# Reordering the second half's routing in a fused mixer and mixture-of-experts kernel, with full-height spread matmuls in the first four groups

## The reference

```
z     = layernorm(layernorm(x))
proj  = (z @ lrp_w.T + lrp_b) * mask * sigmoid(z @ gate_w.T + gate_b)
left, right = split(proj)
tri   = einsum('bikc,bjkc->bijc', left, right)
x1    = x + tri + sigmoid(tri @ og_w.T + og_b) * (layernorm(tri) @ op_w.T + out_bias)
t     = layernorm(x1)
p     = softmax(t @ router_w + router_b);  top 2 of 8, renormalised
out   = x1 + sum over the two of p_e * (t @ expert_w[e] + expert_b[e])
```

## Time and profile before

| | us |
|---|---|
| median of 3 runs (lowest, highest) | 144.69 (143.39, 145.44) |
| the profiled execution's own time | 144.41 |
| its span, first to last instruction | 142.6 |
| busy in the span: TensorE, VectorE, ScalarE, GpSimd | 123.1, 103.6, 76.9, 75.7 |
| mean granted TensorE clock | 0.964 of 2.4 GHz |

### The profile page before, as it was taken

How to read it: one execution, slowest core, us unless ns; L and a number is a source line. 1 busy time by engine, 2 the same in 40 slices (tenths; PEclk the granted TensorE clock), 3 DMA queues, 4 the chain that set the end, 5 groups by cost and what they waited for, 6 DMA issues and landing times. The chain is left out here.

```text
span 142.6 us, 2140 instructions
## 1 busy us (share of the span) xinstructions
PE 123.1 (86%) x708; PEld 53.8 (38%) x711; DVE 103.6 (73%) x173; ACT 76.9 (54%) x136; POOL 75.7 (53%) x73
## 2 busy tenths in 40 slices
PE   5999788999999699889799899695899669989970
PEld 2425145767679565344134443123121111212210
DVE  0096948787774699999918994462978995989951
ACT  4168473565413359898853349858256454474400
POOL 6001033799900089989930173063552974869970
PEclk9999999999999999999999999999559996999999
DMA  4997000000000000000000899987188978871112
GB/s 90 321 350 320 0 0 5 0 0 2 0 5 0 0 2 0 0 5 0 0 0 9 186 208 205 210 187 170 26 202 202 215 182 197 199 283 74 74 74 78
DMA packets 6171, 14.55 MB, mean 102 GB/s; under 512 B 1392, under 2 KB 1648, under 8 KB 6160
## 3 DMA queue, kind: packets, MB, share of 16 engines
q1 hardware_dynamic: 6160, 14.41, 38.1%
HBM read 3.85 MB, written 2.10 MB: 42 GB/s over the span
## 5 line engine op out<-in xcount | busy, mean ns | idle before, releaser
L429 POOL TENSOR_TENSOR work<-work,late_sb 128x512 f32<-128x512 f32 x12 | 15.0, 1274 | 9.7 <-ACT work L526 9.7
L627 ACT ACTIVATE wcopy<-ps 128x512 f32<-128x512 f32 x24 | 13.6, 597 | 9.1 <-PE ps L1024 9.0
L791 PE MATMUL ps<-w1m,xk 64*128 64x256 f32 x128 | 16.2, 391 | 0.8 <-DVE xk L1103 0.3
L1024 PE MATMUL ps<-w3F,selb 32*128 32x512 bf16 x64 | 12.0, 412 | 4.0 <-DVE prod L1306 2.7
L441 POOL TENSOR_TENSOR work<-tri,stats 128x512 f32<-128x512 f32 x8 | 8.8, 1114 | 11.6 <-DVE stats L1172 11.4
L526 ACT ACTIVATE work<-ps 128x512 f32<-128x512 f32 x16 | 9.6, 597 | 9.0 <-PE ps L791 9.0
L491 POOL TENSOR_TENSOR prod<-wcopy,lr 128x512 f32<-128x512 f32 x6 | 8.3, 1405 | 11.3 <-ACT wcopy L627 8.6
L791 PEld LDWEIGHTS ps<-w1m,xk 64*128 64x128 f32 x128 | 11.6, 186 | 5.5 <-DVE lr L1118 2.4
L1118 DVE TENSOR_TENSOR lr<-ps,work 128x512 f32<-128x512 f32 x16 | 10.6, 687 | 2.5 <-POOL work L429 2.5
L1089 DVE TENSOR_SCALAR xk<-ps,head_sb 128x512 f32<-128x512 f32 x8 | 6.4, 798 | 7.4 <-ACT triF L510 7.2
L1024 PEld LDWEIGHTS ps<-w3F,selb 32*128 32x128 bf16 x64 | 3.0, 93 | 20.4 <-issue 6.6
(11 more groups left out here) (136 smaller groups left out, 257.2 us busy)
## 6 DMA issues: line engine op xcount, KB each, us to landing
lr<-triF SPq DMA_DIRECT2D x32, 128.0 KB, 2.3
xi<-in_x_F SPq DMA_DIRECT2D x8, 256.0 KB, 4.6
tri<-triF SPq DMA_DIRECT2D x16, 128.0 KB, 2.4
xk<-triF SPq DMA_DIRECT2D x16, 128.0 KB, 2.3
out<-xi SPq DMA_DIRECT2D x8, 256.0 KB, 2.1
late_sb<-in_late SPq DMA_DIRECT2D x1, 914.0 KB, 7.6
choice_sb<-in_choice SPq DMA_DIRECT2D x1, 336.5 KB, 7.8
early_sb<-in_early SPq DMA_DIRECT2D x1, 257.0 KB, 5.5
```

Source lines behind the costliest of these rows:

```text
L429: pool.tensor_tensor(unit_gates(u), unit_gates(u), mask[:, first_tokens(u)].unsqueeze(1).broadcast_to([P, 2 * C, 8]), ALU.mult).then_inc(s ...
L627: act.activation(wcopy[:, a * W:(a + 1) * W], ps[:, HELD + POOL_N[a] % 4, :], ACT.Copy)\
L791: m = pe.matmul(ps[:, unit_bank(u) + b, 2 * F1 * q:2 * F1 * (q + 1)], xk[rows, at:at + P], w1[rows, 2 * F1 * b:2 * F1 * (b + 1)], start=Tr ...
L1024: pe.matmul(ps[:, HELD + n % 4, :], selb[slot_rows(n % R), n * P:(n + 1) * P], col(w3F, g)[slot_rows(n % R), :], start=True, stop=True).th ...
```

## The change

- tri_squares of groups 4 to 7 run as one block, then x1_copy(1), tri_root(1), x1_copy(3). turn_root(1) and spread_root(1) move ahead of logits(0) and logit_bias(0). spread_root signals for each group instead of once for four.
- VectorE runs tri_scaled(4 to 7) as one block ahead of the comparisons; the gated updates lie each one place earlier between the routing steps.
- The first rounding of half 0 goes ahead of load_roots on ScalarE. TensorE issues out_gate(7) ahead of update(6) and update(7). x1_copy(7) goes from ScalarE to VectorE.
- TensorE's order from turn_weights(1, ...) on is new: all spreads of group 0 and 1 and both sums of group 0 stand ahead of pair_differences(1), and turn_weights(3) is a call of its own. RING follows. VectorE, ScalarE and GpSimd take the products and copies of groups 1 to 3 earlier between the steps of the second half.
- The spreads of groups 0 to 3 take all 128 rows of selb and w3F, those of groups 4 to 7 still 32 rows.

```diff
-                ("g", 7), ("z", 4), ("z", 5), ("z", 6), ("z", 7), ("w", 0), ("var", 1), ("logit", 1), ("w", 1),
-                ("w", 2), ("w", 3), ("std", 1), ("p", 4), ("p", 5), ("p", 6), ("p", 7), ("wins", 1), ("back", 1),
-                ("lead", 1), ("y", 0), ("y", 1), ("w", 4), ("w", 5), ("y", 2), ("y", 3), ("w", 6), ("w", 7), ("y", 4),
+                ("z", 4), ("g", 7), ("z", 5), ("z", 6), ("z", 7), ("w", 0), ("w", 1), ("w", 2), ("w", 3), ("var", 1),
+                ("logit", 1), ("std", 1), ("y", 0), ("p", 4), ("p", 5), ("p", 6), ("p", 7), ("wins", 1), ("back", 1),
+                ("lead", 1), ("y", 1), ("w", 4), ("w", 5), ("y", 2), ("y", 3), ("w", 6), ("w", 7), ("y", 4),
...
-        X1_COPIED_BY_VECTOR = [1, 3, 5]
+        X1_COPIED_BY_VECTOR = [1, 3, 5, 7]
...
             product(0, *POOL_N)
+            product(1, *POOL_N[0:2])
             root_of_each(1)
-            for g in range(1, G):
+            product(1, *POOL_N[2:3])
+            for g in range(2, G):
...
             out_gate(7)
+            round_part(0, 0)
             load_roots()
-            round_part(0, 0)
             x1_square(4)
...
             x1_square(6)
+            w3_copy(0)
             x1_copy(6)
-            w3_copy(0)
             x1_square(7)
-            x1_copy(7)
             weights_copy(0, 0)
+            w3_copy(1)
             weights_copy(0, 1)
             x1_std(1)
-            w3_copy(1)
             weights_copy(0, 2)
             logit_copy(1)
             w3_copy(2)
+            weights_copy(1, 0)
             w3_copy(3)
-            weights_copy(1, 0)
             weights_copy(1, 1)
+            weights_copy(1, 2)
+            weights_copy(2, 0)
             root_back_copy(1)
-            weights_copy(1, 2)
             load_gates()
             probabilities(1)
-            weights_copy(2, 0)
             weights_copy(2, 1)
...
                 for g in range(HG):
-                    m = pe.matmul(ps[:, HELD + g, :], lcp("slot")[slot_rows(g), :], rootF[h][slot_rows(g), :],
-                                  start=True, stop=True)
-                m.then_inc(s_rb, 1)
+                    pe.matmul(ps[:, HELD + g, :], lcp("slot")[slot_rows(g), :], rootF[h][slot_rows(g), :],
+                              start=True, stop=True).then_inc(s_rb, 1)
...
             variance(0)
+            turn_root(1)
             logits(0)
-            turn_root(1)
+            spread_root(1)
             logit_bias(0)
-            spread_root(1)
             pair_differences(0)
...
             lead(0)
+            out_gate(7)
             update(6)
             update(7)
-            out_gate(7)
...
-                    pe.matmul(ps[:, HELD + n % 4, :], selb[slot_rows(n % R), n * P:(n + 1) * P],
-                              col(w3F, g)[slot_rows(n % R), :], start=True, stop=True).then_inc(s_wb, 1)
+
+                    rows = slice(0, P) if g < HG else slot_rows(n % R)
+                    pe.matmul(ps[:, HELD + n % 4, :], selb[rows, n * P:(n + 1) * P], col(w3F, g)[rows, :],
+                              start=True, stop=True).then_inc(s_wb, 1)
...
             spread(0, 2, 3)
+            turn_weights(1, 2)
             variance(1)
+            spread(0, 4, 5, 6, 7)
             logits(1)
-            spread(0, 4, 5, 6, 7)
             logit_bias(1)
-            turn_weights(1, 2, 3)
-            turn_std(1)
             spread_first(1)
             spread(1, 2, 3)
+            turn_std(1)
+            turn_weights(3)
+            spread(1, 4, 5, 6, 7)
+            sum_experts(0, 0)
+            sum_experts(0, 1)
             pair_differences(1)
-            spread(1, 4, 5, 6, 7)
+            spread_first(2)
+            spread(2, 2, 3)
             turn_root_back(1)
             wins(1)
-            sum_experts(0, 0)
+            sum_experts(1, 0)
             lead(1)
-            sum_experts(0, 1)
-            for g in range(2, G):
+            spread(2, 4, 5, 6, 7)
+            sum_experts(1, 1)
+            for g in range(3, G):
...
-                dve.wait_ge(s_rb, g // HG + 1)
+                dve.wait_ge(s_rb, g + 1)
...
-            tri_squares(4)
-            tri_squares(5)
+            for g in range(4, G):
+                tri_squares(g)
             x1_copy(1)
-            tri_squares(6)
-            tri_squares(7)
+            tri_root(1)
             x1_copy(3)
-            tri_root(1)
...
-            tri_scaled(4)
-            tri_scaled(5)
+            for g in range(4, G):
+                tri_scaled(g)
             for n in range(HG):
                 compared(n)
             x1_root(0)
-            tri_scaled(6)
+            gated_update(4)
             top_two(0)
-            tri_scaled(7)
-            gated_update(4)
+            gated_update(5)
             lead_scaled(0)
             top_two_roots(0)
-            gated_update(5)
+            gated_update(6)
             weigh(0)
-            gated_update(6)
+            gated_update(7)
             remainder(0, 0)
-            gated_update(7)
+            closed(7)
             remainder(0, 1)
-            closed(7)
             x1_copy(5)
-            product(0, *VECTOR_N)
-            product(1, *VECTOR_N[0:2])
+            product(0, VECTOR_N[0])
+            x1_copy(7)
+            product(0, *VECTOR_N[1:5])
+            product(1, *VECTOR_N)
             x1_root(1)
+            add_x1(0)
             for n in range(HG, G):
                 compared(n)
-            product(1, VECTOR_N[2])
             top_two(1)
-            product(1, *VECTOR_N[3:5])
+            product(2, *VECTOR_N[0:2])
             lead_scaled(1)
             top_two_roots(1)
-            add_x1(0)
+            product(2, VECTOR_N[2])
             weigh(1)
-            product(2, *VECTOR_N[0:2])
+            add_x1(1)
+            product(2, VECTOR_N[3])
             remainder(1, 0)
-            product(2, *VECTOR_N[2:4])
+            product(2, VECTOR_N[4])
+            product(3, VECTOR_N[0])
             remainder(1, 1)
-            product(2, VECTOR_N[4])
-            add_x1(1)
-            product(3, *VECTOR_N)
+            product(3, *VECTOR_N[1:5])
```

## The result

The changed kernel takes 148.34 us (median of 4 runs, 147.65 to 148.94), the kernel before 144.24 in the same comparison: ratio 1.029, interval 1.024 to 1.035, slower. The profiled execution took 148.84 us with a span of 147.0, against 144.41 and 142.6.

A forecast was written before the change was run, and what follows sets the result against it. Product engines are nearly full from group 4 on, so group 4's start, set by second-half routing, decides: 3.9 less 3.0 plus 0.25 plus 0.3 is 1.45, about 145.9 us; range 142.6 to 148.4.

The forecast's parts named there:

- a rival that didn't come about: Slower side: clock falls in the first stretch too, at 100.85 to 104.9; plus 2.5, 148.4 us, chance 0.20.
- to group 4: From the last rounding's end to group 4's first product: 6.05 us instead of 5.75, plus 0.3.
- The frame: Last stage from group 4's first product stays 18.33 us; the change can only move when group 4 starts.
- The walk's steps: Four engines' queues carried forward instruction by instruction with earlier durations; group 4 starts at 123.3 instead of 121.83.
- The clock at 100: Full-row matmuls hold the clock, so pair_differences(1) to lead_scaled(1) takes 5.9 us instead of 8.87: minus 3.0.
- minus 0.5: First half: first rounding ahead of the table load, so first weights reach w3F at 90.65 instead of 91.11.
- come out even: First half: pair_differences(0) and the comparisons end at 79.0 both before and after the change.
- difference at pair_differences(1): Second half's routing: pair_differences(1) starts at 103.2 instead of 99.30, plus 3.9, with the earlier 0.5 gain used up.
- To the last rounding ... plus 0.25: From lead_scaled(1) to the last rounding's end: 8.15 us instead of 7.9, with add_x1(1) ahead of remainder(1,0).
- Never falls: Clock stays full after 90, group 4 starts near 121.9: plus 0.1, 144.5 us, chance 0.15.
- the order gave less, not more: Rival that order gives more: waits ahead of pair_differences(1) not paid, start about 100.5; 141.0 us, chance 0.12.
- The drains: TensorE ahead of pair_differences(1): five layout switches at about 0.14 us, 0.7 us of the 3.9.

The follow-up runs named there:

- kernel 12: The kernel before with full-row spreads in groups 0 to 3 and half 0's first rounding ahead of out_gate(7) and the table load: 142.66 us, ratio 0.986.
- kernel 6: The changed kernel with 15 matmuls on ones added between group 3's first spreads and ahead of turn_weights(4,5): 146.04 us, ratio 1.009.
- Kernel 1: The changed kernel with all spreads back on 32 rows: 148.28 us, ratio 1.026 to before.
- kernel 7: The changed kernel with VectorE's add_x1(1) moved behind remainder(1,0) and product(2,7), product(3,1) behind remainder(1,1): 146.00 us, ratio 1.008.
- kernel 2: The kernel before with only the spreads of groups 0 to 3 on all 128 rows: 142.99 us, ratio 0.989.
- kernel 10: The changed kernel with add_x1(1) late and 9 added matmuls, none directly ahead of turn_weights(4,5): 144.89 us, ratio 1.002.
- kernel 14: The kernel before with full rows, early first rounding, early group 1 spreads, plus the changed order ahead of the pairs (logits(1) late): 142.25 us, ratio 0.985.
- kernel 4: The changed kernel with pair_differences(1) ahead of both sums of group 0, and comparisons ahead of add_x1(0): 151.15 us, ratio 1.033.
- kernel 13: The kernel before with full rows, early first rounding, and group 1's spreads ahead of turn_std(1): 141.00 us, ratio 0.976.
- kernels 8: The changed kernel with 15 matmuls added around group 3's first spreads and add_x1(1) late: 146.89 us, ratio 1.016.
- kernels 11: The kernel before, 32-row spreads, with 22 matmuls added: 7 ahead of turn_std(1), 15 around group 3's first spreads: 145.50 us, ratio 1.002.
- kernel 9: The changed kernel with 15 added matmuls, add_x1(1) late, and 32-row spreads in all groups: 149.00 us, ratio 1.031.

## Why the prediction was wrong

The forecast was 145.9 us, within 2% of before (0.68 of the chances); the kernel is slower by 2.9%, and its time, 148.34, lies just inside the range's upper end of 148.4. That end was the price of a rival that didn't come about, so the agreement is luck. The step that failed is the term "to group 4", above all the spreads of group 3 priced at full clock. Point by point:

- **The frame held.** The end is group 4's start plus 18.33 us, to the hundredth. The walk's steps through the queues are in the trace, VectorE's wait at add_x1(1) (112.7 forecast, 114.07 found) and turn_std(1) waiting for w3_copy(2) (98.2; 99.45) among them.
- **The clock at 100.** Right: it stays up with full rows, and pair_differences(1) to lead_scaled(1) shrinks by 2.78 us, forecast 3.0.
- **"minus 0.5", gates and rounding.** Wrong in sign: w3F of group 0 came 0.68 us later (91.79). 0.33 of this was there before the first changed instruction (60.78 against 60.45). The first half's logits stand behind spread_root(1): the comparisons started 0.52 us later from the first tri_scaled, where I had written "come out even". From there to w3F only 0.17 was gained; kernel 12, with the rounding ahead of out_gate(7) too, gains 0.37. With the 0.5 us that I had counted on, this makes 1.1 us of the 3.0 us missed, almost all of the difference at pair_differences(1) (5.12 for 3.9).
- **"To group 4 ... plus 0.3".** This term failed most: 1.94, so 1.64 missed. That the clock would fall again was right, and kernel 6 shows it is the cause. The size was not: I let the clock return ahead of the spreads of group 3. It stayed at 0.50 for 6.4 us, and the full-row spreads, which I had priced at 0.22 each, cost 1.89 us together, with sums of 1.94 and 1.88 on either side. The price of the full rows was taken at full clock, while the same text placed them behind the fall of the clock. Kernel 1 gives this price by a run: with 32-row spreads, and the clock low as well, the stretch takes 6.50 us instead of 7.69, so 1.2 of the 1.94 are the full rows. In the three other runs, with a clock of 0.988, this part is smaller; the spans say by some 0.8 to 1.1 us.
- **"To the last rounding ... plus 0.25".** Right in size (0.15). But the stretch held a wait that the change had brought: kernel 7, without it, is 1.35 us shorter there.
- **The rivals.** None came. ("Never falls" has a slip: 1.6 us less on the path gives 121.7 and not 121.9, which decides nothing.) The clock didn't fall early, it did fall late, and the order gave less, not more. The slower side was put on the wrong stretch: the same mechanism (low clock doubling what is on the path) at 118 instead of 100.
- **The drains.** Five switches of layout at 0.14 us fit in the walk: from the first w3F to pair_differences(1) it had 12.55 us with them, and 12.63 were found. No experiment took them apart; the Trainium skill's rule (TensorEngine Tiling (Array Packing), Key Properties) stays a rule with which the trace agrees.

Of the loss against kernel 2, some 5.3 us by the medians, kernel 10 accounts for 3.4 by the late clock and add_x1(1) together. The rest arises ahead of the pairs, which start 43.64 us behind the first tri_scaled in kernel 10 and 40.23 in kernel 2. Of this, kernel 14 shows 1.02 for part of the order, in another kernel; whether the sums of group 0 ahead of the pairs cost anything by themselves stays open, since kernel 4 only moved them to another place of the same chain.

## What to carry to other kernels

Price an instruction at the clock that your own forecast gives it: where matmuls are made larger to hold TensorE's clock, ask what they cost in the stretch where the clock falls anyway. In a chain of steps through in-order queues, useful work belongs where the engine already waits (kernel 13), and moving it from one side of a step to the other (kernel 4) gains nothing. An addition that only frees a bank belongs behind the step that others wait for (kernel 7), and matmuls added for the clock must end before the next input arrives (kernels 8 and 10). Compare a kernel that holds the clock by other means with one that has it anyway (kernels 11 and 2): the same clock didn't give the same time.

## What the runs showed that I had not expected

- Taking work ahead of time can lower the clock. The changed order did the sums of group 1 earlier and so left 5.5 us with 2.4 us of TensorE work ahead of 118.5, and the clock fell; in kernel 2, with the same full-row spreads and the old order, TensorE was busy 4.4 of the 5.5 us ahead of turn_weights(4,5) (109.7 to 115.2), and the clock was 1.00. Kernel 6 fills the stretch, and the clock stays up.
- Matmuls added for the clock can miss it. In kernel 9 the clock fell as they began, five of them took 1.88 us where five take 1.24 at full clock, and turn_weights(4,5) waited behind them. In kernels 6, 8 and 10 the same matmuls found the clock up, and it stayed up.
- The clock of one kernel differs between its executions: the runs in kernel 7's ratio had mean clocks from 0.984 to 1.00.
